# Moving the experts, the output projection and the two norms of one batch to other slots of the next batch's cross attention

## The reference

```
x = layernorm(x + self_attention(x))        # two maps: softmax part and a "memory" part
x = layernorm(x + cross_attention(ctx, x))  # softmax(q k / sqrt(512)) v, then @ Wo.T + bo
x = layernorm(x + ffn(x))                   # top 2 of 8 gates; experts 0 and 1:
                                            # silu(x @ w.T + b) * gate weight, where chosen
```

## Time and profile before

| | us |
|---|---|
| median of 3 runs (1803.44 to 1814.86) | 1807.82 |
| profiled execution, own time | 1807.97 |
| profiled execution, span of the instructions | 1806.2 |
| cross phase, first score to last instruction | 910.8 to 1806.2 |
| batches of the cross phase, first to seventh | 93.1, 101.2, 106.4, 106.4, 106.4, 106.4, 106.4 |

### The profile page before, as it was taken

The page is one execution under the profiler, slowest core; times in us unless marked ns, Lnnn a source line. Parts: engine busy times, 40 slices in busy tenths (PEclk is TensorE's granted clock), DMA queues, the critical chain, the costliest instruction groups (busy, mean ns, idle before and its releaser), DMA issues.

```text
span 1806.2 us, 30853 instructions
## 1 busy us (share of the span) xinstructions
PE 1710.4 (95%) x10602; PEld 1112.9 (62%) x10602; DVE 1266.0 (70%) x2792; ACT 980.7 (54%) x1931; POOL 1181.3 (65%) x969
## 2 busy tenths in 40 slices
PE   5999999999999889999988899999999999999997
PEld 4666666666666547877853456565565656556566
DVE  5677677676777657777856776767767676776744
ACT  3555555555555532433345566565656655566554
POOL 2556556565564554754467887887788687778873
PEclk9999999999999869999988999999999999999999
DMA  7455565565554464576625544435434443543200
GB/s 203 137 157 161 141 160 158 143 165 145 152 154 125 122 206 131 197 204 184 189 73 145 148 107 109 117 86 138 106 99 114 117 109 86 146 107 83 72 35 24
DMA packets 167272, 237.29 MB, mean 131 GB/s; under 512 B 22086, under 2 KB 73286, under 8 KB 167116
## 3 DMA queue, kind: packets, MB, share of 16 engines
q1 hardware_dynamic: 167116, 235.31, 47.1%
HBM read 91.57 MB, written 41.94 MB: 74 GB/s over the span
## 4 chain that ended last, share of the span: by engine, by line
PE 65%; POOL 14%; DVE 7%; issue 5%; ACT 4%; DMA 3%; SPq 1%; POOLq 0%; ACTq 0%; DVEq 0%
POOL cross_added L1920 9%; PE bank L201 8%; PE bank L1606 7%; PE bank L202 6%; PE bank L203 6%; PE bank L296 5%; PE bank L351 5%; PE bank L338 4%; PE bank L1447 4%; PE bank L1418 4%; PE bank L1479 3%; DVE cross_negmax L1428 2%; PE bank L316 2%; DVE bank L1761 2%; PE bank L899 1%
## 5 line engine op out<-in xcount | busy, mean ns | idle before, releaser
L1428 DVE TENSOR_REDUCE cross_negmax<-bank 128x1 f32<-128x512 f32 x512 | 339.7, 676 | 156.2 <-PE bank L1418 151.6
L530 DVE CUSTOM_DVE_ANT_0 bank<-bank,future 128x128 f32<-128x128 f32 (+3 forms) x512 | 246.8, 489 | 172.3 <-PE bank L338 171.6
L1690 ACT ACTIVATE cpt<-bank 128x512 f32<-128x512 f32 x512 | 296.5, 595 | 129.9 <-PE bank L1447 126.4
L412 ACT ACTIVATE pt<-bank 128x256 f32<-128x256 f32 (+3 forms) x512 | 224.5, 441 | 256.8 <-PE bank L296 256.2
L1920 POOL TENSOR_TENSOR cross_added<-cross_added,cpt 128x2048 f32<-128x2048 f32 x64 | 293.5, 4587 | 14.5 <-ACT cpt L1690 14.1
L1447 PE MATMUL bank<-cqk 98*128 98x512 f32 x512 | 228.7, 447 | 24.7 <-ACT cpt L1690 23.8
L594 POOL TENSOR_SCALAR_AFFINE_SELECT pt<-pt 128x512 f32<-128x512 f32 x128 | 81.4, 636 | 252.5 <-ACT pt L412 252.5
L1418 PE MATMUL bank<-cqk 96*128 96x512 f32 x512 | 211.4, 416 | 15.9 <-DVE cross_negmax L1428 13.2
L1920 POOL TENSOR_TENSOR cross_added<-cpt,cpt 128x2048 f32<-128x2048 f32 x32 | 146.8, 4588 | 96.5 <-ACT cpt L1690 96.4
L201 PE MATMUL bank<-xt_hi,w_hi 128*128 128x512 f32 x384 | 168.7, 439 | 16.5 <-DVE w_lo L488 13.6
L296 PE MATMUL bank<-qk 98*128 98x256 f32 (+2 forms) x512 | 181.3, 358 | 2.0 <-ACT pt L412 1.6
(11 more groups left out here) (203 smaller groups left out, 3665.1 us busy)
## 6 DMA issues: line engine op xcount, KB each, us to landing
qk<-stage SPq DMA_DIRECT2D x384, 128.0 KB, 2.3
cqk<-cstage SPq DMA_DIRECT2D x384, 128.0 KB, 2.4
scratch_memory<-memory SPq DMA_DIRECT2D x32, 512.0 KB, 3.8
ma<-scratch_memory SPq DMA_DIRECT2D x32, 512.0 KB, 4.0
raw<-in_x_t SPq DMA_DIRECT2D x32, 256.0 KB, 2.8
v<-in_x SPq DMA_DIRECT2D x32, 256.0 KB, 3.2
scratch_y_ar<-y_ar SPq DMA_DIRECT2D x32, 256.0 KB, 2.2
my_ar<-scratch_y_ar SPq DMA_DIRECT2D x32, 256.0 KB, 4.4
```

The source lines that it names most:

```text
L412: act.activation(s.pt[step % 3][:, j, 0:SEQ - first], sh.bank[2 + n % 2][:, first - q0:SEQ - q0], ACT.Exp, scale=SCALE_SELF).then_inc(s.ac ...
L530: dve.tensor_tensor_reduce(out=scores, in0=scores, in1=sh.future[:, SEQ - P * (qt + 1):SEQ], scale=-1.0, scalar=-NEG, op0=ALU.add, op1=ALU ...
L1428: dve.reduce_max(s.negmax[gm % 2][:, col:col + 1], max_bank(sh, m)[:, :], AX, negate=True).then_inc(s.dve_max, 1)
L1690: act.activation(s.pt[step % 3][:, j, :], sh.bank[2 + n % 2][:, :], ACT.Exp, scale=SCALE_CROSS).then_inc(s.act_exp, 1)
```

## The change

Only tables and the two places that read them are changed: nothing is computed that was not before, and nothing is left out. The experts begin at slot 44 rather than 48 and so end in slot 3 of the following batch rather than slot 7. The 16 chunks of the projection, which stood in slots 12 to 27 in order, now stand as three chunks of row tile 0 in slots 4 to 6, three of row tile 1 in 7 to 9, their last chunks in 15 and 16, and row tiles 2 and 3 in 17 to 24. Additions, norms, transposes, gate, splits, stores and loads of the residual get new slots to suit.

```diff
-PROJECT, FACTORS, APPLY, TRANSPOSE = 12, (18, 22, 26, 30), (20, 24, 28, 32), (25, 29, 31, 34)
-GATE, LOGITS, EXPERT = 38, 43, 48
-LOAD_X1 = (6, 12, 18, 24)
-STATS3, FACTORS3, APPLY3, STORE = (62, 68, 74, 80), (63, 69, 75, 81), (65, 71, 77, 83), (66, 72, 78, 84)
+PROJECT = {4: (0, 0), 5: (0, 1), 6: (0, 2), 7: (1, 0), 8: (1, 1), 9: (1, 2), 15: (0, 3), 16: (1, 3), 17: (2, 0),
+           18: (2, 1), 19: (2, 2), 20: (2, 3), 21: (3, 0), 22: (3, 1), 23: (3, 2), 24: (3, 3)}
+ADD, FACTORS, APPLY, TRANSPOSE = (16, 17, 21, 25), (18, 19, 23, 27), (20, 22, 26, 30), (24, 27, 31, 33)
+GATE, LOGITS, EXPERT = 37, 42, 44
+LOAD_X1 = (6, 13, 15, 21)
+STATS3, FACTORS3, APPLY3, STORE = (58, 64, 68, 76), (59, 65, 69, 78), (66, 71, 73, 81), (67, 72, 74, 82)
...
-Y_HIGH, Y_LOW = (34, 50, 64, 75), (35, 51, 67, 75)
+Y_HIGH, Y_LOW = (36, 48, 60, 74), (37, 51, 66, 75)
...
 def cross_batch(pe, second, s, cw, sh, b, slot):
-    if PROJECT <= slot < PROJECT + TILES * GROUPS:
-        k, c = divmod(slot - PROJECT, GROUPS)
+    if slot in PROJECT:
+        k, c = PROJECT[slot]
...
 def cross_batch_vector(dve, s, sh, b, slot):
-    k, r = divmod(slot - PROJECT - GROUPS, GROUPS)
-    if 0 <= k < TILES and r == 0:
+    if slot in ADD:
+        k = ADD.index(slot)
...
-    if 0 <= k < TILES and r == 1:
+    if slot - 1 in ADD:
+        k = ADD.index(slot - 1)
```

## The result

The changed kernel takes 1796.12 us (median of 6 runs, 1790.53 to 1800.35), the kernel before beside it 1810.78 (6 runs): a ratio of 0.9922, 95% interval 0.9902 to 0.9942. The forecast was 1793. In the profiled execution the span falls from 1806.2 to 1793.7 us, by 12.5; the medians differ by 14.7, and single runs of either kernel spread over some 10.

The account below looks back on a forecast made before the run. POOL was taken to bound slots 8 to 21, PE's issue the rest. Six batches -12.8, batch 1 0, end -3.5, clock +1.5 sum to -14.8: from 1807.97 to 1793 us, range 1781 to 1806.

Parts of the forecast that it names:

- POOL binds slots 8 to 21, PE's issue the rest: Slots 8 to 21: POOL's unbroken run causes 3.36 us of PE waits, shrinking to some 0.4; elsewhere PE's issue binds.
- A new wait of 1.2 for DVE in slots 26 to 28: Slots 26 to 28: 11.6 us of DVE work ends at 46, PE reaches slot 28's maximum at about 44; wait 1.2.
- Slot 37 at 57.3: Slot 37 starts at 57.3, before 63.66, set by POOL's addition ending at 56.25; PE with DVE's wait alone 56.2.
- Slots 37 to 63 at 46.95: Slots 37 to 63: 17 matmuls add 3.96 to 42.78, slot 43's wait 0.2 more; gate margin holds; together 46.95.
- Batch 104.3, six of them -12.8: Batches 2 to 7, taken as alike: 57.3 + 46.95 = 104.3, -2.1 each, six batches -12.8.
- Batch 1 at 0, bounds of 1.5: Batch 1 gets 17 matmuls net and loses the same waits: between -1.5 and +1.5, taken as 0.
- The residual's load behind the stack: SP queue: slot 21's load stands behind the stack's 12 DMAs; cost nothing, 1 per batch if stack slips over 1.5.
- The end at -3.5: After the last score: POOL's 1.63 wait and 1.29 expert addition gone, start 0.6 sooner: -3.5, bounds -1.3 and -4.5.
- The clock at +1.5: New waits in slots 28 and 36 may bring half speed: one in four or five of seven batches at 0.4, +1.5.
- One: Rival: waits of slots 26 to 36 don't come; batch 102.0 to 103.1, whole 1778 to 1787; chance 0.18.
- Two: Rival: what slots 8 to 21 give comes back; batch 105.4, 1799, or 1806 if other margins go; chance 0.20.
- Three: Rival: thinned slots 10 to 14 and 25 to 36 let the clock fall, costing 24; 1816; chance 0.10.

Follow-up runs that it names:

- the light: Kernel before, POOL's two expert additions of slots 8 and 11 cut to one column in batches 0 to 6: 1796.59 us, ratio 0.9916.
- the heavy POOL: Changed kernel plus four spare POOL additions of 128x256 per batch in slots 8 and 11: 1812.3 us, ratio 1.0013 to the kernel before.
- POOL out of the way: Changed kernel with only POOL's subtraction for the keys' low half moved from slot 30 to 33: 1797.71 us, ratio 0.9944.
- the kernel with emptied slots 4 to 11: Kernel before with experts four slots sooner, projection chunks left in slots 12 to 27: 1804.77 us, ratio 0.9975.
- the last kernel: Changed kernel with batch 1's residual load in slot 16, last row tile's steps later, key's subtraction in slot 33, side-by-side run: 1789.19 us, ratio 0.9896.

## Why the prediction was right, point by point

- **POOL binds slots 8 to 21, PE's issue the rest.** Right for the two waits for exponentials, 2.2 of the 3.36 us, shown from both sides by the light and the heavy POOL; the wait for DVE in slot 11 (1.06) is not POOL's, as the light one shows. Addition forecast at 15.65, found at 15.39; slot 22 forecast at 36.2, found at 36.12 (1353.59). The remaining wait, put at 0.4, is 0.11. The expert additions, put at nothing in the gap ahead of that addition, did fit, with 1.21 of 5.20 us to spare.
- **A new wait of 1.2 for DVE in slots 26 to 28.** Right: 1.14 in slot 28, from the order that was counted out. The two stamps given for it, 46 and 44, differ by 2, and how 1.2 comes of them isn't said; PE's maximum there stood ready at 44.5 and began at 45.7.
- **Slot 37 at 57.3, decided by POOL's addition, where PE and DVE alone would be there at 56.2.** The time was right (57.52), the reason not: that is luck. POOL's addition ends at 56.37, as forecast (56.25), but PE reaches its sum at the same moment: it starts at 1374.00 with no wait. With POOL out of the way the slot stays at 57.48. The term that failed is PE's own work in slots 22 to 36, put at 18.8 and measured at 19.78: ten fewer matmuls (nine in the records, of which some are missing) took off 1.3 us, not 2.3; DVE's 0.23 in slot 36 came on top. The 1.7 us said to be given back are 1.4 by the forecast's own figures, and enter no sum.
- **Slots 37 to 63 at 46.95.** 46.31: PE's busy time rose by 3.73 for the 17 matmuls, not by 3.96, the 0.20 of waits from before went, and the 0.2 more for a wait in slot 43 did not come. No wait in slot 47: the gate's margin held.
- **Batch 104.3, six of them -12.8.** 103.83 (103.83 to 105.22), five -11.33 and the sixth -1.35: -12.68. The premise that batches 2 to 7 are alike holds for 2 to 6 only: batch 7 has no row maxima left to make in its last 22 slots and took 98.18 before. That the six come to the forecast is luck: a steady batch won 2.61 and not 2.1, and the clock took the difference back in batches 3 and 7.
- **Batch 1 at 0, bounds of 1.5.** The one term outside its bounds: +3.44. The 17 matmuls came (PE's busy time rose by 4.81, 0.85 more than 3.96; in slots 22 to 36 it fell by 0.15 only, where batch 4 lost 1.32, with the granted clock at 0.87 instead of 0.93). The step "loses the same waits" was wrong. Windows of the kernel before show slots 8 to 21 and 22 to 36 of batch 1, and one of the changed kernel its slots 22 to 36:

```profile
1014.85:1038.47 23.62, 22.09 (x109) 12.76 (x108) 16.30 (x27) 12.66 (x23) 18.71 (x10) 1.00 0.49 138
1038.47:1062.36 23.89, 22.27 (x113) 12.36 (x111) 19.41 (x34) 16.18 (x30) 21.59 (x19) 0.93 0.43 112
```

```profile
1036.49:1062.04 25.55, 22.12 (x103) 11.57 (x102) 18.72 (x32) 16.16 (x31) 20.94 (x15) 0.87 0.41 104
```

  In slots 8 to 21 there were 1.53 us of waits, not 3.36, and all of them for DVE: no experts stand behind batch 1's first slots, so POOL had no expert additions in slots 8 and 11 and never was late. There was less to win, and the new waits of slots 27 and 28 (2.02 and 1.15) brought the waits of slots 22 to 36 from 1.62 to 3.43: over the batch the waits fell from 5.13 to 3.76 where about 4 were counted as gone.
- **The residual's load behind the stack, "1 per batch if the stack slips by over 1.5".** The mechanism came, in batch 1 only, at 1.41 for DVE, and was worth 0.4 of the batch when taken away, no more than the batch varies by. In batch 4 the stack began 0.8 later than forecast (30.5 in the batch) and the addition came as forecast (42.35 for 42.3).
- **The end at -3.5.** -3.15.
- **The clock at +1.5.** It was put as falls in four or five of seven batches at 0.4 us each (1.6 to 2.0). Found were fewer falls, each dearer. Batch 3 lost 1.4 us (105.22 against 103.83), batch 7 about 2 (96.83, against 94.77 in the run with the load moved, which has no such stretch there), and both lost the same when the kernel ran again (105.22 and 96.73). What batch 1's stretch cost by itself no run shows. In the kernel before, the wait of slot 11 is followed by half speed in batches 2, 3 and 7, and batches 2 and 3 took no longer for it (106.44 and 106.40). The window of batch 3, with a granted clock of 0.66, a mix of 2.4 and 1.2 GHz:

```profile
1231.00:1236.00 5.00, 4.38 (x16) 2.24 (x16) 3.41 (x7) 3.35 (x7) 4.71 (x4) 0.66 0.02 3
```

  A fall thus cost a batch nothing where POOL's run bound, and 1.4 to 2 us where PE's own line did.
- **The rivals.** One (no waits in slots 26 to 36) did not come, and in none of the orders tried: what DVE gives back, POOL and ACT take; the best batch was 103.27, against its 102.0 to 103.1. Two decided nothing at full size, but batch 1 is a piece of it. Three needed the clock to fall after both new waits of each batch; it fell in three of seven. The thinned slots 10 to 14, which have no wait, ran at 1.00 (the window of slots 8 to 21 above). In the kernel with emptied slots 4 to 11, half speed followed waits of only 0.64 and 0.27 us (and two more in batch 6) in six batches of six, PE being busy for 3.94 of the 5 us of the first window shown there. The page TensorE: Matmul & The Clock Gate of the Trainium skill (Part 1: The HAM clock gate) has the clock set by how busy PE has been; that run agrees with it.

Which wait is followed by half speed is not settled. With the changed kernel's order, the wait of about 1.15 us in slot 28 (in batch 1 behind one in slot 27) was followed by it in batches 1, 3 and 7 in both executions of the changed kernel, in batch 1 alone with the load moved, and in batches 1 and 5 with the key's subtraction moved alone: nine batches of 28. With the last row tile later, no batch from 1 to 6 fell in three executions, but where the key's subtraction was later too, one batch from 2 to 6 fell in each of three executions, behind waits of 0.41 to 0.43 us in slot 27 and 0.35 in slot 28; other batches with the same two waits did not. One that did, batch 5 of the last kernel, whose second wait ends at 1464.09:

```profile
1464.00:1469.00 5.00, 4.91 (x22) 2.66 (x22) 3.44 (x9) 2.66 (x5) 4.86 (x2) 0.66 0.02 3
```

Against the sum of -14.8 the span fell by 12.5 (the medians by 14.7). The six batches came to -12.68 with the clock's cost in them, where the forecast had -12.8 and +1.5 for the clock, so 1.4 more was won there; batch 1 cost 3.4 more than forecast, and the end gave 0.35 less. Batch 0 (-2.24) and the start of the phase (+2.09), which the change doesn't touch, happen to cancel here.

## What to carry to other kernels

When several engines walk through one list of slots, ask of each moved operation which engine's unbroken run it leaves and which it joins; here 2.7 us of POOL's work moved by four slots brought most of the gain, though PE was the busiest engine, and only together with PE's own work that filled the emptied slots. A steady batch's saving must not be booked for the first batch: look at what stands behind it there. And once a wait was gone, the next engine's run was within a microsecond here: three engines (DVE, POOL, ACT) took turns in slots 28 to 37 as each was relieved.

## What was not expected of the hardware

Batch 0 of the cross phase has the same PE instructions in all these kernels, yet took from 90.78 to 98.88 us in their profiled executions. The granted clock goes with it in part. The windows of batch 0 in the changed kernel, and in the first run with the key's subtraction later:

```profile
912.86:1003.70 90.84, 77.66 (x339) 38.82 (x339) 61.31 (x100) 53.74 (x100) 72.27 (x35) 0.92 0.47 128
```

```profile
914.24:1013.12 98.88, 83.13 (x340) 41.86 (x339) 61.46 (x100) 53.72 (x100) 72.52 (x35) 0.86 0.43 118
```

DVE, ACT and POOL are as busy in both; PE takes 5.5 us longer at a mean of 0.86 instead of 0.92. In between the two don't keep step: 93.08 us at 0.89 in the kernel before, 94.97 at 0.91 with the last row tile later. A spread of 8 us in one batch is nearly as wide as that of the changed kernel's runs (1790.53 to 1800.35), which is why the batches told more than a single time. What decides, in one execution or another, how long PE stays at half speed there was not tried.
